# Gated cross-attention and ternary FFN on one Trainium2 core: quantised rows transposed by DMA in place of TensorE, a pipeline one tile deeper, and the down product in another place

## The chip, the cores and the metric

The kernel runs on one core of one Trainium2 chip. The metric is device microseconds per run. The kernel before takes 1334.1 us, the median of 3 runs (1331.85 to 1337.51). Five engines of the core work side by side, each through its own queue in order: TensorE (matrix products into PSUM), VectorE, ScalarE (activations), GpSimd, and SyncE, which issues the DMAs. They wait for one another on semaphores.

## The reference

x is 4 x 2048 x 512 in float32, the context 4 x 77 x 384; `g_xattn` and `g_ffn` are scalars.

```
x = x + tanh(g_xattn[0]) * xattn(layernorm(x), ctx)     # 8 heads of 64, keys 77, softmax; then @ Wo + bo
x = x + tanh(g_ffn[0])   * ffn(layernorm(x))

def act_quant(x):      # per row
    scale = 127 / clip(max|x|, 1e-5);  return clip(round(x * scale), -128, 127) / scale
def weight_quant(w):   # whole matrix, ternary
    scale = 1 / clip(mean|w|, 1e-5);   return clip(round(w * scale), -1, 1) / scale
bitlinear(x, w) = act_quant(x) @ weight_quant(w).T
g = bitlinear(x, w_gate); u = bitlinear(x, w_up)        # 512 -> 2048
h = relu(g)**2 * u
ffn = bitlinear(h, w_down)                               # 2048 -> 512
```

## The kernel before

The 8192 rows are 64 tiles of 128 rows, 16 tiles to a batch. A preparation makes the ternary weights (held in bf16, w_gate, w_up and w_down) and folds the query weights into the keys and the output weights into the values, batch by batch. Attention then is, for a tile: scores of 8 heads x 77 keys = 616 columns, softmax, five transposes of the probabilities, and a product with the folded values. Scores and attention run in float32r, each operand split into a high and a low part (24 score matmuls of 308 columns, 15 attention matmuls of 512). The FFN's quantised integers are exact in bf16.

The order is written out by hand. Each engine has a function `step(s)`, one for each tile t; `s.has(d)` guards the work for tile t+d, and a step treats several tiles at once. In the kernel before, TensorE's step is: gate and up of tile t, quarters 0 and 1; transposes of the probabilities of t+1 (L950); quarters 2 and 3 (L975); attention of t+1 (L962); three quarters of the scores of t+2 (L58); eight transposes of the first half of the marked hidden row (L983); the rest of the scores; the other eight; the down product (L1002) up to its last four matmuls; four transposes of the marked input of t+1 (L989); the last four of down. A quarter is 512 columns of gate and 512 of up, and its two banks of `gu_ps` alternate with those of the next quarter; the transposes also go to `gu_ps`.

ScalarE's step: relu (L870) and square (L874) of quarters 0 and 1, the high part of the transposed probabilities (L880), quarters 2 and 3, the high part of x (L841), `mark_hidden` (L891), `unmark_hidden` (L896), `mark_input` (L902), `exponentials` of t+2 (L863). Marking multiplies by the row's scale and adds a large constant, so that the rounded integer stands in the low half of the float32 word; the transposes on TensorE take these low halves as bf16, and unmarking subtracts the mark from the 16-bit integers in PSUM and writes bf16 for the next product.

VectorE's step: for each quarter the product with up (L1082) and its maximum (L1085); the low part of the probabilities (L1072); statistics (L1046); the hidden scales (L1091 to L1099); `add_attention` (L1106 on), `unmark_hidden` (L1139), `input_scale`, the maximum and the shift of the scores of t+2 (L1053, L1059), `unmark_input` (L1144), sum, reciprocal and normalisation of the probabilities of t+2 (L1063, L1065, L1068), and `finish` (L1151), which writes y. GpSimd does two roots (L820) and the low part of x (L803) in a step, and splits the folded keys and values at each change of batch (L809, L815). SyncE issues in a step the load of `xf_sb`, of `x_sb`, and the store of y.

Of the kernel before, what the change touches and what calls it, by code (L numbers as in the profile page):

```python
# [11 lines left out]
I16 = mybir.dt.int16  # L12

P = 128
# [7 lines left out]
PAIRS = TILES // 2  # L22
BATCH_PAIRS = TILES_PER_BATCH // 2
# [11 lines left out]
QUARTERS = FFN // 512  # L35
# [10 lines left out]
LOW_MARK = 16384.0  # L46
MARKED = ROUND + LOW_MARK

# [20 lines left out]
def gated_block(nc, x_tok, x_feat, ctx_t, wk, wv, wq_t, wo, bo, gates, wg_t, wu_t, wd_t, out, a_scr, v_scr):  # L69
# [7 lines left out]
    with ExitStack() as keep:  # L77
# [5 lines left out]
        kept.ident_b = sb("ident_b", [P, P], BF16)  # L83
# [37 lines left out]
def prepare(nc, x_tok, x_feat, ctx_t, wk, wv, wq_t, wo, bo, gates, wg_t, wu_t, wd_t, a_scr, v_scr, kept):  # L121
# [3 lines left out]
    ident_f, ident_b, neg_half, w_gate, w_up = kept.ident_f, kept.ident_b, kept.neg_half, kept.w_gate, kept.w_up  # L125
# [7 lines left out]
    with ExitStack() as ctx:  # L133
# [47 lines left out]
        ones_ready, zeros_ready, idents_zeroed = sem("ones_ready"), sem("zeros_ready"), sem("idents_zeroed")  # L181
        idents_ready = sem("idents_ready")
# [27 lines left out]
        with nc.Block() as block:  # L210
# [39 lines left out]
            @block.gpsimd  # L250
            def _(pool):
                nc.gpsimd.memset(ones[:, :], 1.0).then_inc(ones_ready, 1)
                nc.gpsimd.memset(k_pairs[:, :, :, :], 0.0).then_inc(zeros_ready, 1)
                nc.gpsimd.memset(v_pairs[:, :, :], 0.0).then_inc(zeros_ready, 1)
                nc.gpsimd.memset(neg_half[:, :], -0.5)
                nc.gpsimd.memset(ident_f[:, :], 0.0).then_inc(idents_zeroed, 1)
                nc.gpsimd.memset(ident_b[:, :], 0.0).then_inc(idents_zeroed, 1)
                pool.wait_ge(idents_zeroed, 2)
                for m in (ident_f, ident_b):
                    nc.gpsimd.affine_select(out=m[:, :], in_=m[:, :], compare_op=ALU.not_equal, fill=1.0, base=0,  # L260
                                            pattern=[[-1, P]], channel_multiplier=1).then_inc(idents_ready, 1)
# [294 lines left out]
def run_tiles(nc, x_tok, x_feat, out, a_scr, v_scr, kept):  # L556


    ident_f, ident_b, neg_half = kept.ident_f, kept.ident_b, kept.neg_half
# [7 lines left out]
    x_tok = x_tok.rearrange("(k o) p d -> k o p d", o=2)  # L567
    x_feat = x_feat.rearrange("(k o) p c t -> k o p c t", o=2)
    out = out.rearrange("(k o) p d -> k o p d", o=2)

    with ExitStack() as ctx:
# [3 lines left out]
        def sem(name):  # L575
# [11 lines left out]
        x1 = sb("x1", [P, 2, DIM], F32)  # L587
# [15 lines left out]
        hidden_scale = sb("hidden_scale", [P, 1], F32)  # L603
        x_marked = sb("x_marked", [P, DIM], F32)
        xq_t = sb("xq_t", [P, DIM], BF16)
        quarter_max = sb("quarter_max", [P, QUARTERS], F32)
# [4 lines left out]
        y_scale = sb("y_scale", [P, 1], F32)  # L611


        relu, relu_sq, y_sb = (staged[:, at:at + FFN // 2].rearrange("p (s n) -> p s n", s=2)
                               for at in (0, FFN // 2, 5 * FFN // 2))
        hidden = staged[:, FFN:2 * FFN]
        hq_t = staged[:, 2 * FFN:5 * FFN // 2].bitcast(BF16)
# [9 lines left out]
        ht_ps = [gu_ps[:, 0, n, :].bitcast(BF16) for n in range(2)]  # L627
        xt_ps = gu_ps[:, 1, 0, 0:DIM // 2].bitcast(BF16)
        x_bits = x_marked[:, :].bitcast(BF16).rearrange("p (n two) -> p n two", two=2)
        h_bits = h_marked[:, :].bitcast(BF16).rearrange("p (n two) -> p n two", two=2)  # L630
# [19 lines left out]
        xt_done, xq_ready = sem("xt_done"), sem("xq_ready")  # L650
        top_n_done, top_sq_done, hidden_scale_done = sem("top_n_done"), sem("top_sq_done"), sem("hidden_scale_done")
        gu_done = [sem(f"gu_done{n}") for n in range(QUARTERS)]
        relu_done = [sem(f"relu_done{n}") for n in range(QUARTERS)]
        square_done = [sem(f"square_done{n}") for n in range(QUARTERS)]
        hidden_done = [sem(f"hidden_done{n}") for n in range(QUARTERS)]
        quarter_max_done = sem("quarter_max_done")
# [3 lines left out]
        ht_done = [sem(f"ht_done{n}") for n in range(2)]  # L660
        hq_ready = [sem(f"hq_ready{n}") for n in range(2)]
# [5 lines left out]
        class Step:  # L667
# [3 lines left out]
            def __init__(self, eng, k, o, values=()):  # L671
                self.k, self.o, self.fixed = k, o, isinstance(k, int)
                self.held = {}
                if not self.fixed:
                    self.held = {c: 2 * k + (o + c) for c in values}
# [3 lines left out]
            def count(self, c):  # L679

                return self.held[c] if c in self.held else 2 * self.k + (self.o + c)
# [10 lines left out]
            def pair(self, d):  # L692
                return self.k + (self.o + d) // 2

            def loads(self, d):

                return 16 * self.pair(d) + 16

            def batch_chunks(self, d, chunks):

                return chunks * (self.pair(d) // BATCH_PAIRS) + chunks

            def opens(self, t):

                return self.fixed and 2 * self.k + self.o == t

            def has(self, d):
                return not self.fixed or 0 <= 2 * self.k + self.o + d < TILES

        SP_VALUES = (1, 2, 3)  # L710
# [5 lines left out]

        def steps(eng, step, values):

            for t in (-1, 0, 1):
                step(Step(eng, t // 2, t % 2))  # L720
            with eng.Fori(1, PAIRS - 2) as k:
                for o in range(2):
                    step(Step(eng, k, o, values))
            for t in range(TILES - 4, TILES):
                step(Step(eng, t // 2, t % 2))

        def steps_by_batch(eng, step, values, split_keys, split_values):

            for t in (-1, 0, 1):
                step(Step(eng, t // 2, t % 2))  # L730
            with eng.Fori(1, BATCH) as b:
                with eng.Fori(1, BATCH_PAIRS - 1) as k:
                    for o in range(2):
                        step(Step(eng, (b - 1) * BATCH_PAIRS + k, o, values))
                k = (b - 1) * BATCH_PAIRS + (BATCH_PAIRS - 1)
                split_keys(b)
                step(Step(eng, k, 0, values))
                split_values(b)
                step(Step(eng, k, 1, values))
                for o in range(2):  # L740
                    step(Step(eng, k + 1, o, values))
            with eng.Fori(PAIRS - BATCH_PAIRS + 1, PAIRS - 2) as k:
                for o in range(2):
                    step(Step(eng, k, o, values))
            for t in range(TILES - 4, TILES):
                step(Step(eng, t // 2, t % 2))

        with nc.Block() as block:
            @block.sync
            def _(sp):  # L750
# [8 lines left out]
                def load_xf(s, d):  # L759
                    sp.dma_start(xf_sb[:, s.par(d), :, :], x_feat[s.pair(d), s.par(d)]).then_inc(xf_loaded[s.par(d)], 16)  # L760

                def load_x(s, d):
                    sp.dma_start(x_sb[:, s.par(d), :], x_tok[s.pair(d), s.par(d)]).then_inc(x_loaded[s.par(d)], 16)

                def step(s):
                    if s.has(4):

                        sp.wait_ge(xf_low_done, s.through(2))
                        load_xf(s, 4)
                    if s.has(3):  # L770

                        sp.wait_ge(x1_done, s.through(1))
                        load_x(s, 3)
                    if s.has(0):

                        sp.wait_ge(x1_done, 1)
                        sp.wait_ge(y_done, s.through(0))
                        sp.dma_start(out[s.pair(0), s.par(0)], y_sb[:, s.par(0), :]).then_inc(y_stored[s.par(0)], 16)
# [3 lines left out]
                step(Step(sp, -1, 1))  # L782
                with sp.Fori(1, BATCH) as b:
                    load_folded(b)
                    with sp.Fori(0, BATCH_PAIRS) as k:
                        for o in range(2):
                            step(Step(sp, (b - 1) * BATCH_PAIRS + k, o, SP_VALUES))
                with sp.Fori(PAIRS - BATCH_PAIRS, PAIRS - 2) as k:
                    for o in range(2):
                        step(Step(sp, k, o, SP_VALUES))  # L790
                for t in range(TILES - 4, TILES):
                    step(Step(sp, t // 2, t % 2))
                for n in range(2):
                    sp.wait_ge(y_stored[n], 16 * PAIRS)

            @block.gpsimd
            def _(pool):
# [23 lines left out]

                def step(s):
                    if s.has(2):
                        root(var1_ready, s, 2, rstd1, var_eps1, rstd1_done)
                    if s.has(1):
                        root(var2_ready, s, 1, rstd2, var_eps2, rstd2_done)
                    if s.has(3):
                        low_part(s, 3)
# [3 lines left out]
                split_values(0)  # L832
                steps_by_batch(pool, step, (2, 3, 4), split_keys, split_values)

            @block.scalar
            def _(act):
# [28 lines left out]
                def square_quarter(s, n):  # L865
                    wait(act, gu_done[n], s.through(0))
# [3 lines left out]
                    nc.scalar.activation(relu[:, n % 2, :], gu_ps[:, n % 2, 0, :], ACT.Relu).then_inc(relu_done[n], 1)  # L870
                    wait(act, relu_done[n], s.through(0))

                    wait(act, hidden_done[(n + 2) % 4], s.count(1 if n >= 2 else 0))
                    nc.scalar.activation(relu_sq[:, n % 2, :], relu[:, n % 2, :], ACT.Square).then_inc(square_done[n], 1)  # L874
# [7 lines left out]
                def mark_hidden(s):  # L882
                    wait(act, h_scale_done, s.through(0))

                    wait(act, ht_done[1], s.before(0))
                    if s.opens(0):

                        wait(act, weight_done, PIECES)
                    for n in range(2):
                        cols = slice(n * FFN // 2, (n + 1) * FFN // 2)  # L890
                        nc.scalar.activation(h_marked[:, cols], hidden[:, cols], ACT.Copy, bias=MARKED,  # L891
                                             scale=h_scale[:, 0:1]).then_inc(h_marked_done[n], 1)

                def unmark_hidden(s):
# [344 lines left out]
```

## Time and profile before

| | before |
|---|---|
| median of 3 runs | 1334.1 us |
| lowest, highest | 1331.85, 1337.51 us |
| profiled execution: span, first to last instruction | 1332.6 us |
| busy TensorE | 1281.4 us, 96% |
| busy VectorE | 1123.8 us, 84% |
| busy ScalarE | 754.0 us, 57% |
| busy GpSimd | 199.7 us, 15% |
| mean granted TensorE clock | 0.990 |
| DMA traffic | 82.46 MB, mean 62 GB/s |

The profiled execution's own time is known by its span alone, which is 1.5 us under the median. The busy shares count instructions that overlap once. In the slices of the page, each of 40 equal parts of the span has a digit for the tenths that an engine is busy; PEclk is the TensorE clock that was granted, in tenths of full speed. A row of the timeline gives the start, the length and the instruction group, and in brackets the engine's idle time ahead of it with what ended it. Lengths of matmuls overlap: the start of one to the start of the next is what the engine spends.

### The profile page before, as it was taken

The page shows a single profiled execution, that of the slowest core. Times are in us where ns is not written, and L with a number is a line of the kernel's source. Part 1 is how long each engine was busy: PE and PEld are TensorE (multiplying, and loading weights), DVE is VectorE, ACT ScalarE, POOL GpSimd, SP SyncE. Part 2 cuts the span into 40 slices and gives each one's busy share as a digit, 9 for nine tenths or more (in the row PEclk, how much of TensorE's full clock was granted, in tenths as well). Part 3 has the DMA queues.
Part 4 walks back from the last instruction along what each step waited for, and adds up shares of the span by engine and source line. Part 5 has one row for each costly group of instructions (what it writes and reads, how often), then busy time and mean ns, then how long its engine had stood idle before and what let it go on. Part 6 is the DMA issues. An engine that isn't in the chain of part 4 may idle for free.

```text
span 1332.6 us, 21398 instructions
## 1 busy us (share of the span) xinstructions
PE 1281.4 (96%) x7289; PEld 848.3 (64%) x7416; DVE 1123.8 (84%) x2462; ACT 754.0 (57%) x1038; POOL 199.7 (15%) x216
## 2 busy tenths in 40 slices
PE   7768999999999999999999999999999999999996
PEld 5535666666666666666666666666666666666663
DVE  4969888888888888888888888888888888888885
ACT  3754555555566555555566555555566555555554
POOL 1022011101132111111122111111122110111000
PEclk9889999999999999999999999999999999999999
DMA  9732111111113111111112211111111111111100
GB/s 391 258 130 100 43 46 39 39 47 40 42 37 121 42 39 39 47 39 45 34 47 88 68 38 47 39 47 32 47 39 45 34 47 39 47 31 47 31 25 17
DMA packets 35188, 82.46 MB, mean 62 GB/s; under 512 B 3946, under 2 KB 3946, under 8 KB 32609
## 3 DMA queue, kind: packets, MB, share of 16 engines
q1 hardware_dynamic: 34589, 78.03, 17.2%
q10 hardware_dynamic: 580, 4.20, 1.0%
q8 instruction: 9, 0.15, 0.1%
q14 instruction: 10, 0.08, 0.0%
HBM read 57.86 MB, written 24.35 MB: 62 GB/s over the span
## 4 chain that ended last, share of the span: by engine, by line
PE 86%; DVE 3%; issue 2%; ACT 1%; POOL 0%; ACTq 0%; DVEq 0%; POOLq 0%
PE gu_ps L975 31%; PE o_ps L962 16%; PE y_ps L1002 16%; PE s_ps L58 16%; PE gu_ps L983 4%; PE s_ps L950 2%; PE gu_ps L989 1%; ACT v_sb L854 1%; DVE staged L1158 0%; ACT staged L891 0%; DVE probs L1059 0%; DVE staged L1082 0%; POOL v_sb L815 0%; DVE score_max L1053 0%; DVE w_down L1160 0%
## 5 line engine op out<-in xcount | busy, mean ns | idle before, releaser
L870 ACT ACTIVATE staged<-gu_ps 128x512 f32<-128x512 f32 x256 | 153.1, 598 | 230.9 <-PE gu_ps L975 230.5
L975 PE MATMUL gu_ps<-w_gate,xq_t 128*128 128x512 bf16 x961 | 259.3, 379 | 4.5 <-DVE xq_t L1144 0.9
L975 PE MATMUL gu_ps<-w_up,xq_t 128*128 128x512 bf16 x1024 | 262.8, 379 | 0.0
L1002 PE MATMUL y_ps<-w_down,staged 128*128 128x512 bf16 x960 | 228.5, 380 | 3.6 <-issue 0.2
L891 ACT ACTIVATE staged<-staged,h_scale 128x1024 f32<-128x1024 f32 x128 | 140.3, 1144 | 148.9 <-DVE h_scale L1098 148.9
L820 POOL TENSOR_TENSOR rstd<-var_eps,neg_half 128x1 f32<-128x1 f32 x128 | 74.1, 579 | 994.7 <-DVE var_eps L1048 647.0
L1082 DVE TENSOR_TENSOR staged<-staged,gu_ps 128x512 f32<-128x512 f32 x256 | 174.9, 683 | 53.1 <-ACT staged L874 53.0
L962 PE MATMUL o_ps<-v_sb,pt_high 128*128 128x512 f32 (+1 forms) x640 | 213.4, 415 | 3.4 <-DVE pt_low L1072 2.9
L58 PE MATMUL s_ps<-a_sb,xf_high 128*128 128x308 f32 x1024 | 191.4, 309 | 0.0
L1085 DVE TENSOR_REDUCE quarter_max<-staged 128x1 f32<-128x512 f32 x256 | 175.6, 686 | 8.8
L975 PEld LDWEIGHTS gu_ps<-w_up,xq_t 128*128 128x128 bf16 x1024 | 100.2, 98 | 120.8
L874 ACT ACTIVATE staged<-staged 128x512 f32<-128x512 f32 x256 | 161.7, 632 | 8.2
L975 PEld LDWEIGHTS gu_ps<-w_gate,xq_t 128*128 128x128 bf16 x1024 | 92.6, 97 | 111.5 <-DVE staged L1082 19.7
L58 PEld LDWEIGHTS s_ps<-a_sb,xf_high 128*128 128x128 f32 x1024 | 157.2, 188 | 5.8 <-issue 0.5
L1002 PEld LDWEIGHTS y_ps<-w_down,staged 128*128 128x128 bf16 x1024 | 95.0, 98 | 91.6 <-issue 1.0
L962 PEld LDWEIGHTS o_ps<-v_sb,pt_high 128*128 128x128 f32 (+1 forms) x640 | 121.1, 190 | 37.5 <-DVE pt_low L1072 3.2
L962 PE MATMUL o_ps<-v_sb,pt_low 128*128 128x512 f32 (+1 forms) x320 | 127.1, 397 | 0.0
L896 ACT ACTIVATE staged<-gu_ps 128x1024 bf16<-128x1024 int16 x64 | 65.5, 1024 | 101.4 <-PE gu_ps L983 101.4
L58 PE MATMUL s_ps<-a_sb,xf_low 128*128 128x308 f32 x512 | 113.3, 302 | 0.0
L983 PE MATMUL gu_ps<-ident_b,staged 128*128 128x128 bf16 x1024 | 80.4, 222 | 8.3 <-ACT staged L891 8.3
L58 PEld LDWEIGHTS s_ps<-a_sb,xf_low 128*128 128x128 f32 x512 | 84.5, 189 | 0.0
L803 POOL TENSOR_TENSOR xf_low<-xf_sb,xf_high 128x512 fp32r<-128x512 f32 x62 | 79.0, 1275 | 0.0
(112 smaller groups left out, 1509.3 us busy)
## 6 DMA issues: line engine op xcount, KB each, us to landing
xf_sb<-in_x_feat SPq DMA_DIRECT2D x64, 256.0 KB, 2.6
x_sb<-in_x_tok SPq DMA_DIRECT2D x64, 256.0 KB, 2.6
y<-staged SPq DMA_DIRECT2D x64, 256.0 KB, 2.0
staged<-in_wg_t SPq DMA_DIRECT2D x4, 1024.0 KB, 15.3
staged_up<-in_wu_t SPq DMA_DIRECT2D x4, 1024.0 KB, 23.2
staged<-in_wd_t ACTq DMA_DIRECT2D x4, 1024.0 KB, 7.1
a_scr<-a_out SPq DMA_DIRECT2D x12, 308.0 KB, 4.4
a_raw<-a_scr SPq DMA_DIRECT2D x3, 1232.0 KB, 5.3
```

The costliest lines, as they stand in the source:

```text
L58: last = nc.tensor.matmul(s_ps[:, n, 0:HALF_KEYS], x_part[:, c, :], a_sb[:, a, c, n * HALF_KEYS:(n + 1) * HALF_KEYS], start=(c == 0 and x_ ...
L803: nc.gpsimd.tensor_tensor(xf_low[:, s.par(d), :, :], xf_sb[:, s.par(d), :, :], xf_high[:, s.par(d), :, :].bitcast(F32), ALU.subtract).then ...
L820: nc.gpsimd.tensor_tensor(rstd[:, :], var_eps[:, :], neg_half[:, :], ALU.pow).then_inc(done, 1)
L870: nc.scalar.activation(relu[:, n % 2, :], gu_ps[:, n % 2, 0, :], ACT.Relu).then_inc(relu_done[n], 1)
L874: nc.scalar.activation(relu_sq[:, n % 2, :], relu[:, n % 2, :], ACT.Square).then_inc(square_done[n], 1)
L891: nc.scalar.activation(h_marked[:, cols], hidden[:, cols], ACT.Copy, bias=MARKED, scale=h_scale[:, 0:1]).then_inc(h_marked_done[n], 1)
L962: last = nc.tensor.matmul(o_ps[:, :], pt[0:rows, P * c:P * (c + 1)], v_sb[0:rows, v, c, :], start=(c == 0 and pt is pt_high and v == 0), s ...
L975: last = nc.tensor.matmul(gu_ps[:, n % 2, m, :], xq_t[:, P * c:P * (c + 1)], w[:, c, 512 * n:512 * (n + 1)], start=(c == 0), stop=(c == DC ...
L983: last = nc.tensor.transpose(ht_ps[n][:, P * c:P * (c + 1)], h_bits[:, at:at + P, 0], ident_b[:, :])
L1002: last = nc.tensor.matmul(y_ps[:, :], hq_t[:, P * c:P * (c + 1)], w_down[:, c, :], start=(c == 0), stop=(c == FC - 1))
L1082: nc.vector.tensor_tensor(hidden[:, cols], relu_sq[:, n % 2, :], gu_ps[:, n % 2, 1, :], ALU.mult).then_inc(hidden_done[n], 1)
L1085: nc.vector.tensor_reduce(quarter_max[:, n:n + 1], hidden[:, cols], axis=AX, op=ALU.max, apply_absolute_value=True).then_inc(quarter_max_d ...
```

## The change

Hidden row and input are no longer transposed on TensorE. Marking now adds `ROUND` alone; unmarking subtracts it from SBUF and writes bf16 rows (`hq` in halves, by VectorE and ScalarE; `xq` by VectorE); SyncE transposes these rows from SBUF to SBUF with `dma_start_transpose` (`turn_hidden`, two a tile, 128x1024 each; `turn_input`, one, 128x512) into `hq_t` and `xq_t`. The down product of a tile is in the step behind its gate and up (`down(s, -1)`), and `finish` in the one behind that (`finish(s, -2)`). `x1` becomes a ring of four, `hidden_scale`, `y_scale` and `xq_t` rings of two.

Gate and up come in two halves instead of four quarters. A half is 1024 columns of gate and then 1024 of up and fills the four banks of `gu_ps`; relu, square, product and maximum are one instruction a half. Relu waits for the gate product alone (`gate_done`), the product with up for `up_done`. The multiplication of the probabilities by the reciprocal sum goes from VectorE to GpSimd. Loops are unrolled over four tiles instead of two, and the split of keys and values at a change of batch stands two steps later in them.

```
 def gate_up(s, n):
+    wait(pe, hidden_done[1 - n], s.count(n))
+    for m, w, done in ((0, w_gate, gate_done), (1, w_up, up_done)):
+        for q in range(2):
+            cols = slice(HALF * n + 512 * q, HALF * n + 512 * (q + 1))
+            for c in range(DC):
+                last = nc.tensor.matmul(gu_ps[:, m, q, :], xq_t[:, s.par(0), c, :], w[:, c, cols], ...)
+        last.then_inc(done[n], 1)
 # TensorE
 def step(s):
-    gate_up(s, 0); gate_up(s, 1)
     transpose_probs(s, 1)
-    gate_up(s, 2); gate_up(s, 3)
+    gate_up(s, 0)
     attend(s, 1)
-    make_scores(s, 2, range(DC - 1)); transpose_hidden(s, 0); make_scores(s, 2, range(DC - 1, DC))
-    transpose_hidden(s, 1); down(s, range(FC - DC)); transpose_input(s, 1); down(s, range(FC - DC, FC))
+    make_scores(s, 2)
+    down(s, -1)
+    gate_up(s, 1)
 # ScalarE
 def step(s):
+    probs_high(s, 1); mark_hidden(s, -1)
+    relu_half(s, 0); square_half(s, 0)
+    unmark_hidden(s, -1); high_part(s, 3); mark_input(s, 1)
+    relu_half(s, 1)
+    exponentials(s, 2)
+    square_half(s, 1)
 # VectorE
 def step(s):
+    probs_low(s, 1); finish(s, -2); input_stats(s, 2); unmark_hidden(s, -1)
+    hidden_half(s, 0)
+    add_attention(s, 1); input_scale(s, 1)
+    top_scores(s, 2); unmark_input(s, 1); shift_scores(s, 2)
+    top_half(s, 0); hidden_unit_scale(s, 1); sum_probs(s, 2)
+    hidden_half(s, 1); top_half(s, 1); hidden_scales(s)
 # GpSimd
 def step(s):
     root(var1_ready, s, 2, ...)
+    low_part(s, 3)
     root(var2_ready, s, 1, ...)
-    low_part(s, 3)
+    normalise(s, 2)
 # SyncE
+def turn_hidden(s, d, n):
+    wait(sp, hq_done[n], s.through(d))
+    wait(sp, down_done, s.before(d))
+    sp.dma_start_transpose(hq_t[:, n * FC // 2:(n + 1) * FC // 2, :], hq[:, n * HALF:(n + 1) * HALF]).then_inc(hq_turned[n], 16)
+def turn_input(s, d):
+    wait(sp, xq_done, s.through(d))
+    wait(sp, up_done[1], s.before(d - 1))
+    sp.dma_start_transpose(xq_t[:, s.par(d), :, :], xq[:, :]).then_inc(xq_turned, 16)
 def step(s):
+    wait(sp, y_done, s.through(-2)); sp.dma_start(out[...], y_sb[:, s.par(-2), :])
+    turn_hidden(s, -1, 0); turn_hidden(s, -1, 1)
     load_xf(s, 4); load_x(s, 3)
+    turn_input(s, 1)
```

## Rows read from the trace of the kernel before

**Rows 1.** The page: busy us, share of span and instructions; granted clock in 40 slices.
```profile
PE 1281.4 (96%) x7289; PEld 848.3 (64%) x7416; DVE 1123.8 (84%) x2462; ACT 754.0 (57%) x1038; POOL 199.7 (15%) x216
...
PEclk9889999999999999999999999999999999999999
```

**Rows 2.** TensorE's timeline, 949 to 979 us: start us, us, instruction group.
```profile
954.10 0.71 PE L950 MATMUL s_ps<-ident_f,probs 128*128 128x128 f32 x5
954.64 1.03 PE L975 MATMUL gu_ps<-w_gate,xq_t 128*128 128x512 bf16 x4
...
957.23 1.03 PE L975 MATMUL gu_ps<-w_up,xq_t 128*128 128x512 bf16 x4
...
961.59 0.73 PE L58 MATMUL s_ps<-a_sb,xf_high 128*128 128x308 f32 x4
...
964.14 0.62 PE L983 MATMUL gu_ps<-ident_b,staged 128*128 128x128 bf16 x8
964.57 0.80 PE L58 MATMUL s_ps<-a_sb,xf_high 128*128 128x308 f32 x4
...
966.16 2.54 PE L1002 MATMUL y_ps<-w_down,staged 128*128 128x512 bf16 x11
968.54 0.39 PE L989 MATMUL gu_ps<-ident_b,x_marked 128*128 128x128 bf16 x4
...
973.08 0.71 PE L950 MATMUL s_ps<-ident_f,probs 128*128 128x128 f32 x5
```

**Rows 3.** ScalarE's and VectorE's timeline of the same stretch.
```profile
954.30 0.60 ACT L870 ACTIVATE staged<-gu_ps 128x512 f32<-128x512 f32 x1 [0.47 <-PE gu_ps L975]
...
962.36 2.19 ACT L891 ACTIVATE staged<-staged,h_scale 128x1024 f32<-128x1024 f32 x2 [2.28 <-DVE h_scale L1098]
...
968.29 0.81 ACT L863 ACTIVATE probs<-probs,rstd 128x616 f32<-128x616 f32 x1 [0.51 <-DVE probs L1059]
...
961.48 0.16 DVE L1091 TENSOR_REDUCE h_max<-quarter_max 128x1 f32<-128x4 f32 x1
...
969.87 0.79 DVE L1063 TENSOR_REDUCE prob_sum<-probs 128x8 f32<-128x616 f32 x1
970.69 0.20 DVE L1065 RECIPROCAL prob_inv<-prob_sum 128x8 f32<-128x8 f32 x1
```

**Rows 4.** Groups by line and form, whole run: busy us, mean ns; idle before, releaser.
```profile
L1082 DVE TENSOR_TENSOR staged<-staged,gu_ps 128x512 f32<-128x512 f32 x256 | 174.9, 683 | 53.1 <-ACT staged L874 53.0
L803 POOL TENSOR_TENSOR xf_low<-xf_sb,xf_high 128x512 fp32r<-128x512 f32 x62 | 79.0, 1275 | 0.0
L891 ACT ACTIVATE staged<-staged,h_scale 128x1024 f32<-128x1024 f32 x128 | 140.3, 1144 | 148.9 <-DVE h_scale L1098 148.9
L896 ACT ACTIVATE staged<-gu_ps 128x1024 bf16<-128x1024 int16 x64 | 65.5, 1024 | 101.4 <-PE gu_ps L983 101.4
L815 POOL TENSOR_TENSOR v_sb<-v_raw,v_sb 128x2048 fp32r<-128x2048 f32 x4 | 18.2, 4561 | 16.1 <-ACT v_sb L854 16.1
```

**Rows 5.** DMA view: packets, MB, engine share; issues with KB and us to landing.
```profile
q1 hardware_dynamic: 34589, 78.03, 17.2%
...
xf_sb<-in_x_feat SPq DMA_DIRECT2D x64, 256.0 KB, 2.6
...
y<-staged SPq DMA_DIRECT2D x64, 256.0 KB, 2.0
```

**Rows 6.** TensorE's timeline, first gate and up of the last tile.
```profile
1310.58 1.03 PE L975 MATMUL gu_ps<-w_gate,xq_t 128*128 128x512 bf16 x4
```

**Rows 7.** TensorE's timeline in the preparation; then windows (busy us of each engine, PEclk, DMA).
```profile
56.72 1.31 PE L287 MATMUL s_ps<-k_pairs,wq_sb 128*128 128x154 f32 x8 [1.91 <-ACT a_out L358]
...
76.68 7.54 PE L301 MATMUL v_ps<-wo_sb,v_pairs 128*128 128x512 f32 x13 [3.17 <-DVE v_pairs L464]
...
48.00:60.00 12.00, 8.95 (x43) 6.02 (x43) 11.82 (x13) 10.22 (x11) 0.00 (x0) 1.00 0.97 337
...
76.00:80.00 4.00, 3.32 (x5) 1.50 (x6) 1.90 (x11) 1.29 (x2) 0.56 (x1) 0.65 0.20 78
```

More of the change, by code:

```diff
@@ L626, in run_tiles @@
         pt_ps = s_ps[:, :, :].rearrange("p s n -> p (s n)")
[L627 to L630, printed above, removed]
+        gate_ps = gu_ps[:, 0, :, :].rearrange("p s n -> p (s n)")
+        up_ps = gu_ps[:, 1, :, :].rearrange("p s n -> p (s n)")
         v_parts = ((slice(0, P), slice(0, KC - 1)), (slice(0, LAST_ROWS + 1), slice(KC - 1, KC)))
@@ L674, in __init__ @@
                 if not self.fixed:
-                    self.held = {c: 2 * k + (o + c) for c in values}
+                    self.held = {c: QUAD * k + (o + c) for c in values}
                     for value in self.held.values():
@@ L744, in steps_by_batch @@
                     step(Step(eng, k, o, values))
-            for t in range(TILES - 4, TILES):
-                step(Step(eng, t // 2, t % 2))
+            last_steps(eng, step)
         with nc.Block() as block:
@@ L769, in step @@
                         load_xf(s, 4)
                     if s.has(3):
-                        sp.wait_ge(x1_done, s.through(1))
+                        wait(sp, x1_done, s.through(1))
                         load_x(s, 3)
[L774 to L778, printed above, removed]
+                    if s.has(1):
+                        turn_input(s, 1)
@@ L780, in _ @@
                 start = Step(sp, 0, 0)
                 load_xf(start, 2)
[L782 to L789, printed above, removed]
+                step(Step(sp, -1, QUAD - 1))
@@ new lines, in _ @@
+                for o in range(QUAD):
+                    step(Step(sp, 0, o))
+                    if o == 0:
+                        load_folded(1)
+                with sp.Fori(1, BATCH - 1) as b:
+                    with sp.Fori(1, BATCH_QUADS + 1) as j:
+                        for o in range(QUAD):
+                            step(Step(sp, (b - 1) * BATCH_QUADS + j, o, SP_VALUES))
+                    load_folded(b + 1)
+                with sp.Fori(QUADS - 2 * BATCH_QUADS + 1, QUADS - 1) as k:
+                    for o in range(QUAD):
@@ L968, in gate_up @@
                     if n == 0:
-                        wait(pe, xq_ready, s.through(0))
-                    if n >= 2:
-                        wait(pe, hidden_done[n - 2], s.through(0))
-                    for m, w in enumerate((w_gate, w_up)):
-                        for c in range(DC):
-                            last = nc.tensor.matmul(gu_ps[:, n % 2, m, :], xq_t[:, P * c:P * (c + 1)],
-                                                    w[:, c, 512 * n:512 * (n + 1)], start=(c == 0), stop=(c == DC - 1))
@@ L992, in down @@
-                def down(s, chunks):
-                    for n in range(2):
-                        if n * FC // 2 in chunks:
-                            wait(pe, hq_ready[n], s.through(0))
-                    if 0 in chunks:
-                        if s.opens(0):
-                            wait(pe, weight_done, PIECES)
-                        wait(pe, y_done, s.before(0))
-                    for c in chunks:
-                        last = nc.tensor.matmul(y_ps[:, :], hq_t[:, P * c:P * (c + 1)], w_down[:, c, :],
+                        wait(pe, xq_turned, s.turns(0))
@@ L1003, in down @@
+                def down(s, d):
+                    if s.opens(-d):
+                        wait(pe, weight_done, PIECES)
+                    wait(pe, y_done, s.before(d))
+                    for c in range(FC):
+                        for n in range(2):
+                            if c == n * FC // 2:
+                                wait(pe, hq_turned[n], s.turns(d))
+                        last = nc.tensor.matmul(y_ps[:, :], hq_t[:, c, :], w_down[:, c, :],
                                                 start=(c == 0), stop=(c == FC - 1))
-                    if FC - 1 in chunks:
-                        last.then_inc(down_done, 1)
+                    last.then_inc(down_done, 1)
@@ L1154, in ternary_down, with finish @@
+                def finish(s, d):
+                    wait(dve, down_done, s.through(d))
+                    wait(dve, y_scale_done, s.through(d))
+                    wait(dve, y_stored[s.par(d)], s.loads(d) - 16)
+                    nc.vector.scalar_tensor_tensor(y_sb[:, s.par(d), :], y_ps[:, :], y_scale[:, s.par(d):s.par(d) + 1],
+                                                   x1[:, s.ring(d), :], ALU.mult, ALU.add).then_inc(y_done, 1)
                 def ternary_down(p):
```

348 lines of the change are left out of this document (174 added, 174 removed).

## The prediction, made before the changed kernel ran

> **What bounds the kernel now.** I read the page's busy shares first: TensorE is busy 96% of the span, VectorE 84%, and behind the preparation (the first 110 us) TensorE's granted clock stays at 1.0 [rows 1]. A busy share does not say whether TensorE waits between its groups, so the timeline of one tile in the middle of the run came next [rows 2]. The probability transposes of one tile start at 954.10, those of the next at 973.08: 18.98 us a tile. The pieces, start to start: probability transposes 0.54 (954.10 to 954.64); half of gate and up 3.46 (954.64 to 958.10, where the four matmuls that start at 957.23 have been issued); attention 3.50 (958.10 to 961.59); scores 0.85 for six matmuls, 3.40 for 24; eight hidden transposes 0.43 (964.14 to 964.57), twice; down 16 x 0.217 = 3.48 (eleven take 2.38, from 966.16 to 968.54); four input transposes 0.22; the other half of gate and up 3.46. Their sum is 18.92, and 0.07 comes from breaking the scores in two. So TensorE has work without a hole, and 62 such steps make nearly the whole run. Everything else has slack: the exponential starts at 968.29 and the probabilities are wanted at 973.08 [rows 2, 3].
>
> **What is removed from the bound.** The 16 hidden and 4 input transposes, 0.86 + 0.22, and the break in the scores: TensorE's work falls to 0.54 + 3.46 + 3.50 + 3.40 + 3.48 + 3.46 = 17.84 us. Alone that is 1.14 us a tile. VectorE loses the normalisation (to GpSimd), about 0.8 us, and some fixed parts of instructions; it is not the bound before or after.
>
> **What the new order adds.** Number the step from the start of its probability transposes. TensorE does: transposes of tile t+1, 0.00 to 0.54; first half of gate and up of t, to 4.00; attention, to 7.50; scores of t+2, to 10.90; down of t-1, to 14.38; gate of the second half, to 16.11; up, to 17.84. Two things follow.
>
> First, ScalarE's queue has `relu_half(1)` ahead of `exponentials(2)`. The relu waits for the second gate product, at 16.11, though the scores were done at 10.90 and shifted by VectorE some 2.4 us later. Before, no wait on a late matmul stood there, the exponential waited 0.51 for its own input [rows 3]. Everything behind it is serial and the next step's first TensorE instruction, `transpose_probs`, waits for its end:
> - from the last gate matmul to the start of the relu 0.20 (954.10 against 954.30 in [rows 2, 3]);
> - relu over 128x1024 out of PSUM 1.02 (the row of 1024 elements out of PSUM, [rows 4]);
> - exponential 0.81, started 0.10 early as two of ScalarE's independent instructions overlap (two of 1.144 take 2.19), so 0.71 [rows 3, 4];
> - sum 0.04 + 0.78, reciprocal 0.04 + 0.20 [rows 3];
> - normalisation on GpSimd: no row has it. Its nearest rows are 128x512 in 1.275 and 128x2048 in 4.561, a slope of 2.14 ns an element, so 1.50 for 616 elements [rows 4]. From below it can't be under the 1.275 of fewer elements; from above I allow 2.0 for the broadcast operand. With 0.08 to start and 0.05 to TensorE: 1.63.
> Sum 4.62, so the next transposes start at 16.11 + 4.62 = 20.73. TensorE idles 2.9 us a step, and the step is 1.75 us longer than the 18.98 of before.
>
> Second, a half of gate and up now fills all four banks of gu_ps, where quarters alternated. So the first half of the next tile waits for `hidden_half(1)`: 0.20 + 1.02 + 0.71 + square 1.04 (1.144 less the overlap) + 0.04 + a product over 1024 elements (683 ns for 512, [rows 4], less one fixed part: 1.22) + 0.05 = 4.28, at 20.39. It hides behind the first loop, whose transposes end at 21.27, by 0.88. But had the first loop been free, this one would still give 20.39 - 0.54 = 19.85, slower than before.
>
> **The transposing DMAs.** SyncE issues three more transfers per tile, 256 KB twice and 128 KB, between the store of y and the loads; each such step holds SyncE behind waits for `hq_done`, `down_done` and `xq_done`, and the loads of x behind them, wanted a step later, have slack. When are they due? In the cycle of 20.73, the hidden maximum is done at 0.82, its scale 0.9 later (before, 961.48 to the ScalarE start at 962.36 [rows 3]), at 1.75. ScalarE marks until 3.94 (2.19), VectorE has the first half unmarked by about 5.1 (behind `probs_low`, `finish`, `input_stats`), ScalarE the second, behind relu and square, by about 7.0. Down wants the halves at 10.90 and 12.64. So each transfer has about 5.7 us. The input is ready near 12.5 and wanted at 21.27: 8.8 us. No row shows a transposing transfer. From below: the plain ones of the same bytes take 2.0 to 2.6 us from issue to landing. From above: 78 MB went in 34589 packets that took 17.2% of 16 x 1332.6 us, 106 ns each for 2.3 KB [rows 5]; if every 256-byte row of a transpose cost as much, a half is 1024 / 16 x 106 ns = 6.8 us of all engines and two in a row land near 20.5, which would hold down, and the step, by 7.9 us. I take 4 us, nearer the plain row because the bytes are the same and the engines are 83% idle; then nothing is late.
>
> The Trainium skill ("DMA: Bandwidth & Descriptors", Latency and other measured facts) gives transposing transfers an effective 261 GB/s, some 1.0 us for a half behind a fixed 2 us: by that rule nothing is late either. Against the change speaks "Advanced Engine Details and Errata" (DGE: Hardware vs Software) of the Trainium skill, which calls hardware-generated transposes the less efficient ones; it has no figure, and no row here tests it. It stands beside rival B.
>
> **The ends.** 62 steps at +1.75 are +108. At the three changes of batch GpSimd's split of the values (over 4.6 us and the last chunk behind it, [rows 4]) now starts at about 0.8 of the step whose attention starts at 4.0, not a whole gate and up ahead: about +2.5 each, +8. Input 0 comes through a DMA: +3. Behind the last gate and up the deeper pipeline has a whole down (of tile 62), the second half, and then marking, unmarking, transfer, down, finish and store in a row: I get 31.5 from the start of the last tile's gate and up, where before it was 1332.6 - 1310.6 = 22.0 [rows 6]: +9.5; one short step before it -1.5. Sum +127 on the span of 1332.6: 1460. The runs' median is 1334.1, 1.5 above the span.
>
> **TensorE's clock.** The waits that I add are 2.9 us. Before, after a wait of 3.17 that ended at 76.68 the granted clock is 0.65 over 76 to 80, so 1.2 in place of 2.4 GHz for 2.8 of 4 us; with a wait of 1.91 that ended at 56.72 it stays at 1.00 over 48 to 60 [rows 7]. 2.9 lies between, nearer the side that fell. A fall costs half of the stretch at half speed, over 1.4 us; I take 1.6. From never to every step that is 0 to +99 us; I take a third of the steps, +31. Forecast: 1460 + 31 + 1.5 = 1492 us.
>
> The Trainium skill ("TensorE: Matmul & The Clock Gate", Why this matters for your kernels) warns of idle gaps between bursts of matmuls in mid-kernel. Read strictly, that is rival F; the rows show one gap on either side and leave it open.
>
> **The rivals.** A measurement of this kernel tells 0.5%, about 7 us, from no change.
> - A, the forecast (52%): the softmax tail sets the step, the clock falls in some steps, 1440 to 1530.
> - F, the clock falls in every step (12%): 2.9 us of idle come once a step, and each is enough. 1460 + 62 x 1.6 + 1.5 = 1560. For it the wait that ended at 76.68, against it the one that ended at 56.72 [rows 7].
> - B, transfers late (18%): the transposed halves of the hidden rows land after 12.64, down stands, and as down lies in front of the second gate product, each us later is 62 us. It decides from 5.7 us after the issue. 1.5 us too late: 1492 + 93 = 1585. For it: 256-byte rows, and no measured one; against it: idle engines.
> - C, bound by TensorE, faster (8%): TensorE stays without holes at 17.84 and the removed transposes are kept. It needs the tail behind the second gate product to be no longer than the 1.73 of the up product, not 4.62: the exponential not held up. 1332.6 - 62 x 1.14 + 20 = 1282, where 20 is the ends' 19 and the 1.5 beside the span. Against it: the in-order queue of ScalarE, the four full banks. The side turns at a step of 18.98 - 20/62 = 18.66, a tail of 2.5 us.
> - D (2%): the two cancel, 1327 to 1341.
> - E (8%): only a part of the tail: GpSimd's piece shorter or semaphores quicker, no fall of the clock, 1341 to 1440.
> That the transposes leave TensorE is sure; that they were its bound is too. What is lost is worth more.
>
> Chances: faster 0.08, same 0.02, slower 0.90. The range, 1420 to 1600, leaves out C, D and the far part of B.
>
> **What would show it.** In the timeline after: idle of about 2.9 us before the probability transposes, released by GpSimd's normalisation; a step of 20.7 us where the clock stays at 1.0; the exponential starting right behind a relu of 1.0 us, with ScalarE waiting about 4 us for the gate product; gaps of the granted clock in some steps; no wait of down for a DMA. If down waits for hq_t, B holds. If TensorE's idle ends with VectorE's product in place of GpSimd's, the second loop binds and the step is 19.9. If TensorE is above 98% busy with steps of 17.9, the whole argument is wrong. Clock gaps in every step speak for F, none at all for a run near 1461.

## The result

The changed kernel takes 1465.4 us, median of 4 runs (1464.61 to 1468.81), beside 1335.3 for the kernel before; the ratio is 1.0989, 95% interval 1.0964 to 1.1015. It is 10% slower. The forecast was 1492 us, 12% slower, in a range of 1420 to 1600.

The page of the changed kernel, in the same columns as [rows 1]; the last two lines are its chain of waits, by engine, and its transposing transfers:

```profile
span 1466.9 us, 18673 instructions
...
PE 1237.2 (84%) x6040; PEld 782.6 (53%) x6136; DVE 1064.9 (73%) x2142; ACT 694.0 (47%) x782; POOL 306.3 (21%) x278
...
PEclk9979999999999999999999999999999999999997
...
PE 39%; issue 34%; DVE 11%; POOL 7%; ACT 2%; DMA 1%; DVEq 0%; POOLq 0%; ACTq 0%; SPq 0%
...
hq_t<-staged SPq DMA_TRANSPOSE x128, 3.0
```

TensorE does 44 us less than before and takes 134 us longer: its share falls from 96 to 84%. The chain of waits puts 34% on "issue" and 7% on GpSimd. "Issue" names no cause: it is time for which the chain shows no wait, in a plain step mostly some 8.4 us ahead of GpSimd's normalisation. The waits say more. The two longest waits of TensorE in the changed kernel (us in total, times, longest):

```profile
PE s_ps L1001 <- POOL probs L863: 170.9, 64, 12.2
PE y_ps L1041 <- DMA hq_t<-staged: 14.3, 4, 9.2
```

All 64 tiles wait for GpSimd's normalisation; for a DMA down waits in 4 only. The timeline of one step, TensorE first, then ScalarE, VectorE, GpSimd, to set beside [rows 2, 3]:

```profile
954.56 0.77 PE L1001 MATMUL s_ps<-ident_f,probs 128*128 128x128 f32 x5 [2.45 <-POOL probs L863]
955.16 1.89 PE L1028 MATMUL gu_ps<-w_gate,xq_t 128*128 128x512 bf16 x8
...
965.51 3.63 PE L1041 MATMUL y_ps<-w_down,hq_t 128*128 128x512 bf16 x15
968.98 1.89 PE L1028 MATMUL gu_ps<-w_gate,xq_t 128*128 128x512 bf16 x8
970.70 1.89 PE L1028 MATMUL gu_ps<-w_up,xq_t 128*128 128x512 bf16 x8
...
970.90 1.02 ACT L916 ACTIVATE staged<-gu_ps 128x1024 f32<-128x1024 f32 x1 [4.23 <-PE gu_ps L1028]
971.83 0.80 ACT L909 ACTIVATE probs<-probs,rstd 128x616 f32<-128x616 f32 x1
972.52 1.04 ACT L922 ACTIVATE staged<-staged 128x1024 f32<-128x1024 f32 x1
...
967.14 0.79 DVE L1087 TENSOR_TENSOR probs<-s_ps,score_max 128x616 f32<-128x616 f32 x1
...
972.66 0.80 DVE L1091 TENSOR_REDUCE prob_sum<-probs 128x8 f32<-128x616 f32 x1 [3.02 <-ACT probs L909]
973.49 0.20 DVE L1093 RECIPROCAL prob_inv<-prob_sum 128x8 f32<-128x8 f32 x1
...
973.77 1.22 POOL L863 TENSOR_TENSOR probs<-probs,prob_inv 128x616 f32<-128x616 f32 x1 [8.45 <-DVE prob_inv L1093]
...
975.04 0.77 PE L1001 MATMUL s_ps<-ident_f,probs 128*128 128x128 f32 x5 [2.45 <-POOL probs L863]
```

Read it backwards from 975.04, the next step's start. The normalisation ends at 974.99, started at 973.77 behind the reciprocal, that behind the sum, that behind the exponential at 971.83. The exponential's input was ready at 967.93; it started 3.9 us later because ScalarE stood in front of the relu, 4.23 us, for the last gate matmul, which ends at 970.70. From there to 975.04 is 4.34 us, of which the up product covers 1.73. The step is 975.04 - 954.56 = 20.48. TensorE's idle ahead of the transposes, 2.45 us by its row, is called the hole below.

Over the run, the starts of the probability transposes give the account of the 134.3 us. Plain steps are the 52 behind the first two in which no batch changes:

| | before | after | difference |
|---|---|---|---|
| start to first transposes | 97.4 | 101.0 | +3.6 |
| first two steps | 39.7 | 38.1 | -1.5 |
| 52 plain steps | 18.98 each | 20.48 each | +78.0 |
| 3 changes of batch, 3 steps each | 172.2 | 208.7 | +36.5 |
| from the last transposes to the end | 36.4 | 54.1 | +17.7 |

### The profile page after: what moved, and what is told of

Read it like the earlier page. It is cut to its first block, busy times and chain, and to the rows that moved or that the text cites. A ratio compares the mean times of both kernels' runs of the same rounds, so it can differ in the third digit from the quotient of the medians.

```text
span 1466.9 us, 18673 instructions
## 1 busy us (share of the span) xinstructions
PE 1237.2 (84%) x6040; PEld 782.6 (53%) x6136; DVE 1064.9 (73%) x2142; ACT 694.0 (47%) x782; POOL 306.3 (21%) x278
## 4 chain that ended last, share of the span: by engine, by line
PE 39%; issue 34%; DVE 11%; POOL 7%; ACT 2%; DMA 1%; DVEq 0%; POOLq 0%; ACTq 0%; SPq 0%
PE o_ps L1013 15%; PE gu_ps L1028 15%; POOL probs L863 5%; PE s_ps L1001 3%; PE y_ps L1041 3%; DVE stats L1137 3%; DVE x L1135 3%; PE s_ps L56 2%; POOL rstd L858 2%; DVE centred L1141 2%; POOL v_sb L853 1%; DVE mean_var L1067 1%; ACT staged L922 1%; ACT v_sb L900 1%; DMA hq_t<-staged 1%
## 5 line engine op out<-in xcount | busy, mean ns | idle before, releaser
L916 ACT ACTIVATE staged<-gu_ps 128x1024 f32<-128x1024 f32 x128 | 130.1, 1016 | 276.7 <-PE gu_ps L1028 276.5
L1041 PE MATMUL y_ps<-w_down,hq_t 128*128 128x512 bf16 x962 | 228.4, 385 | 18.3 <-DMA hq_t<-staged 14.3
L1107 DVE TENSOR_TENSOR staged<-staged,gu_ps 128x1024 f32<-128x1024 f32 x128 | 156.0, 1219 | 70.9 <-ACT staged L922 70.9
L1001 PE MATMUL s_ps<-ident_f,probs 128*128 128x128 f32 (+1 forms) x320 | 51.9, 296 | 170.9 <-POOL probs L863 170.9
L863 POOL TENSOR_TENSOR probs<-probs,prob_inv 128x616 f32<-128x616 f32 x64 | 78.8, 1231 | 529.6 <-DVE prob_inv L1093 529.6
L1091 DVE TENSOR_REDUCE prob_sum<-probs 128x8 f32<-128x616 f32 x64 | 50.9, 795 | 190.4 <-ACT probs L909 190.4
L952 ACT ACTIVATE x_marked<-centred,x_scale 128x512 f32<-128x512 f32 x64 | 46.2, 722 | 268.3 <-DVE x_scale L1154 268.3
L1041 PEld LDWEIGHTS y_ps<-w_down,hq_t 128*128 128x128 bf16 x1024 | 96.1, 99 | 130.5 <-issue 19.1
L1112 DVE TENSOR_REDUCE half_max<-staged 128x1 f32<-128x1024 f32 x128 | 155.4, 1214 | 2.2
L922 ACT ACTIVATE staged<-staged 128x1024 f32<-128x1024 f32 x128 | 134.8, 1053 | 2.2
```

What stands on the lines that cost most here:

```text
L863: nc.gpsimd.tensor_tensor(probs_by_head, probs_by_head, inv, ALU.mult).then_inc(probs_ready, 1)
L916: nc.scalar.activation(relu, gate_ps, ACT.Relu).then_inc(relu_done[n], 1)
L922: nc.scalar.activation(relu_sq, relu, ACT.Square).then_inc(square_done[n], 1)
L1001: last = nc.tensor.transpose(pt_ps[0:cols, P * c:P * (c + 1)], probs[:, P * c:P * c + cols], ident_f[:, :])
L1041: last = nc.tensor.matmul(y_ps[:, :], hq_t[:, c, :], w_down[:, c, :], start=(c == 0), stop=(c == FC - 1))
L1107: nc.vector.tensor_tensor(hidden[:, cols], relu_sq, up_ps, ALU.mult).then_inc(hidden_done[n], 1)
```

## The experiments

Theory 1: the order makes two loops, chains that leave TensorE at the second gate product and come back to it, one through the softmax tail and one through the four full banks of `gu_ps`; the removed transposes were worth their full price. Rivals: the transposing transfers; VectorE's long list; the clock.

**The down product behind the second half.** One move in TensorE's step:

```
-    if s.has(-1): down(s, -1)
     if s.has(0):  gate_up(s, 1)
+    if s.has(-1): down(s, -1)
```

> The changed kernel with the down product of the tile before moved behind the second half of gate and up. Theory 1 (the softmax tail behind the second gate product sets the step of 20.48 us, because only the up product of 1.73 us lies beside it): 3.48 us of down now lie beside that tail too, 1.73 + 3.48 is more than the 4.34 that the tail takes, so TensorE has no hole left in plain steps, the step is about 17.9 us and the run 1300 to 1325. Rival (the time went into the transposing DMAs, or into VectorE with its long in-order list): the step stays above 19 us, the run above 1380.

Measured: 1290.0 us, ratio to the kernel before 0.9657 (0.9634 to 0.9680). Plain steps are 17.81 us, the 17.84 that I had added up for TensorE's work. TensorE and GpSimd of this kernel, and a window of one step (us busy of TensorE, its weight loads, VectorE, ScalarE, GpSimd; granted clock):

```profile
871.32 1.90 PE L1028 MATMUL gu_ps<-w_gate,xq_t 128*128 128x512 bf16 x8
873.06 1.89 PE L1028 MATMUL gu_ps<-w_up,xq_t 128*128 128x512 bf16 x8
874.79 3.62 PE L1041 MATMUL y_ps<-w_down,hq_t 128*128 128x512 bf16 x16
878.24 0.71 PE L1001 MATMUL s_ps<-ident_f,probs 128*128 128x128 f32 x5
...
876.38 1.22 POOL L863 TENSOR_TENSOR probs<-probs,prob_inv 128x616 f32<-128x616 f32 x1 [5.34 <-DVE prob_inv L1093]
...
860.40:878.20 17.80, 17.80 (x93) 11.52 (x92) 15.11 (x33) 9.71 (x11) 4.00 (x4) 1.00 0.32 81
```

The normalisation ends at 877.60, 4.54 behind the gate product's end (4.29 in the changed kernel), and 0.64 ahead of the transposes that want it. The same tail is there; down covers it. VectorE's list, 15.11 us, fits. The transfers, the deeper pipeline and the halves are all in this kernel too, and it is faster than the kernel before: without the down product in its place ahead of the second half, none of them makes the kernel slow.

**The exponential ahead of the second relu.**

```
+    if s.has(2): exponentials(s, 2)
     if s.has(0): relu_half(s, 1)
-    if s.has(2): exponentials(s, 2)
```

> The changed kernel with the exponential ahead of the second relu in ScalarE's queue. Theory 1: the exponential starts some 3 us earlier and the probabilities are ready in time; then the second loop binds, relu, square and product of the second half before the next gate product may write the same four banks: the last gate matmul at 16.1, the next first half at 19.7, a step of 19.2 us, the run about 1390. Rival (GpSimd's normalisation alone was late, and the banks cost nothing): 17.9 us a step, 1310. Rival (ScalarE's order is without effect): 1465.

Measured: 1398.9 us, ratio 1.0478 (1.0453 to 1.0503), steps of 19.26. TensorE's timeline has the wait at the place of the second loop, ahead of the first gate product, released by VectorE's product, and none before the transposes:

```profile
870.41 1.89 PE L1028 MATMUL gu_ps<-w_up,xq_t 128*128 128x512 bf16 x8
872.14 0.71 PE L1001 MATMUL s_ps<-ident_f,probs 128*128 128x128 f32 x5
874.13 1.89 PE L1028 MATMUL gu_ps<-w_gate,xq_t 128*128 128x512 bf16 x8 [1.28 <-DVE staged L1107]
```

So the move takes 20.48 - 19.26 = 1.22 us off the step, and the banks hold the other 1.45 down to 17.81. The 1.22 is not the price of the softmax tail alone: the exponential ahead of the relu is out of the second loop too, so both loops got shorter.

**Work put into the hole, and in front of it.** Five matmuls more per tile, 1.08 us, the price of the transposes that were removed: once in the up product of the second half, once in its gate product.

```
 for q in range(2):
+    if n == 1 and m == 1 and q == 1:         # m == 0 in the second kernel
+        for c in (0, 1, 2, 3, 0):
+            nc.tensor.matmul(gu_ps[:, m, q, :], xq_t[...], w[:, c, cols], start=True, stop=True)
```

> The changed kernel with five more matmuls of 512 columns in every second half, in the up product behind the last gate matmul (1.08 us a tile, as much as the transposes that left TensorE; their result is overwritten). Theory 1: they fall into TensorE's hole, the time stays within 0.5% of the changed kernel, 1465. Rival (TensorE's work still counts): up to 64 x 1.08 = 69 us more, 1534.

> The same five matmuls in the gate product of the second half, ahead of the semaphore that releases the relu. Theory 1: this work lies on the loop, so all of it shows: 60 x 1.08 = 65 us more, about 1530. Rival (a hole absorbs it wherever it stands): 1465.

Measured: 1463.6 us behind the gate, steps of 20.48 unchanged; 1587.0 ahead of its end. The first shows that 1.08 us of TensorE's work a tile, as much as was saved, is worth nothing at that place of this order. The second is 122 us more where 65 were expected. In its timeline the hole is as long as ever, but two kinds of step stand side by side, 21.55 and 23.24 (the transposes that open four steps, and windows over two of them with the granted clock in the last column but two):

```profile
1004.73 0.80 PE L1001 MATMUL s_ps<-ident_f,probs 128*128 128x128 f32 x5 [2.44 <-POOL probs L863]
1027.97 0.76 PE L1001 MATMUL s_ps<-ident_f,probs 128*128 128x128 f32 x5 [2.44 <-POOL probs L863]
1051.20 0.77 PE L1001 MATMUL s_ps<-ident_f,probs 128*128 128x128 f32 x5 [2.44 <-POOL probs L863]
1072.75 0.77 PE L1001 MATMUL s_ps<-ident_f,probs 128*128 128x128 f32 x5 [2.44 <-POOL probs L863]
...
1051.20:1072.80 21.60, 19.15 (x98) 11.98 (x98) 15.10 (x33) 9.71 (x11) 4.00 (x4) 1.00 0.26 67
1028.00:1051.20 23.20, 20.76 (x97) 12.33 (x97) 15.14 (x33) 9.71 (x11) 4.03 (x4) 0.93 0.26 62
```

The longer step has the clock at 0.93 of its 23.2 us, 3.2 us at 1.2 GHz, and is 1.69 longer. Of the 52 plain steps 32 are such, 54 us, nearly all of the missing part.

**A third transfer.** 128x1024 more transposed per tile into a tile that nothing reads, ahead of the two:

```
 if n == 0:
+    wait(sp, spare_turned, s.turns_before(d))
+    sp.dma_start_transpose(spare_t[:, :, :], hq[:, 0:HALF]).then_inc(spare_turned, 16)
+    sp.wait_ge(spare_turned, s.turns(d))       # in the second kernel only
```

> The changed kernel with a third transposing transfer of 128x1024 per tile, of the same rows into a tile that nothing reads, queued ahead of the two of the hidden row. In the changed kernel a transfer lands 3.0 us after issue and SyncE spends some 1.4 us on each; down begins 5.3 us after the first issue. Theory 1 (the transfers are hidden, slack over 2 us): it delays the two by about 1.4 us and the time stays within 0.5% of 1465. Rival (the transfers are on the path, by their engines or by contention in SBUF): 1.4 us a tile, 1550.

> The same third transfer, and SyncE waits for its landing before it issues the two: a delay of 3.0 us. Theory 1 with the slack as read (first half lands at 8.6 of the step and is due at 10.9, the second at about 10.2 and due at 12.7): down waits some 0.5 to 0.9 us a tile, 1495 to 1525. Rival (there is more slack): 1465. Rival (already on the path): 3 us a tile, 1650.

Measured: 1472.5 without the wait (ratio 1.1047, 1.1016 to 1.1079), 0.5% above the changed kernel, where 1.4 us a tile would be 6%; plain steps are 20.48 as before. So the transfers of the hidden rows, and half as many again, stay hidden in plain steps. The last 0.5% is at the edge of what the runs can tell. Of the 3.3 us between the two profiled executions 3.2 lie behind the last probability transposes (57.3 us against 54.2), where down has to wait for its transfers. With the wait 1548.3, outside what I expected. TensorE's waits of that kernel:

```profile
PE s_ps L1009 <- POOL probs L871: 169.7, 64, 12.2
PE y_ps L1049 <- DMA hq_t<-staged: 59.2, 40, 12.4
```

Its steps are 21.24 where the clock stays up, +0.76, within the 0.5 to 0.9 read from the slack; but 31 of the 52 plain steps are longer, up to 22.36, with the clock at half speed 27 times between 170 and 1490 us; the changed kernel has no such plain step. The slack was right, the clock was again what I had left out.

**The normalisation back on VectorE.**

```
 nc.vector.reciprocal(prob_inv, prob_sum)
+nc.vector.tensor_tensor(probs_by_head, probs_by_head, inv, ALU.mult)     # and out of GpSimd's step
```

> The changed kernel with the multiplication by the reciprocal sum back on VectorE, behind the reciprocal. Theory 1: the softmax tail gets shorter by 0.4 us (about 0.84 in place of 1.23 and two hand-offs), but the product of the second half, which VectorE does next, starts 0.84 later and frees the banks at the moment at which the first half of the next tile starts now: the second loop takes over, the step stays 20.4 to 20.6 us, the run 1455 to 1475. Rival (GpSimd's share of the tail counts in full): 20.0 us, 1435.

Measured: 1496.2 us, ratio 1.1213 (1.1185 to 1.1242): slower, where no change was expected. The timeline has the second loop behind the first, as reasoned: a wait before the transposes, then 0.45 more for VectorE's product.

```profile
604.31 0.77 PE L998 MATMUL s_ps<-ident_f,probs 128*128 128x128 f32 x5 [1.99 <-DVE probs L1093]
605.53 1.89 PE L1025 MATMUL gu_ps<-w_gate,xq_t 128*128 128x512 bf16 x8 [0.45 <-DVE staged L1107]
...
624.96 0.77 PE L998 MATMUL s_ps<-ident_f,probs 128*128 128x128 f32 x5 [1.99 <-DVE probs L1093]
```

The step is 20.65, +0.17, 9 us over the 52. The rest is the clock: 20 of the 52 plain steps are longer, most 22.3 or 21.8, 28 us in all. These 37 us are more than the 27.6 between the profiled executions, because this kernel reaches its first transposes at 92.2 us instead of 101.0.

**One matmul more.** Three kernels with longer steps had falls of the clock in plain steps, the changed kernel had none. In two of the three its hole was nearly unchanged (2.44 us, and 1.99 with 0.45 behind it); in the one with the waited transfer, waits of down came beside it. The diff is the one above with m == 0 and `for c in (0,)`.

> The changed kernel with one more matmul of 512 columns (0.22 us) in the gate product of the second half. TensorE's hole stays 2.45 us a step, only the step gets longer, 20.70. Theory 3 (in the changed kernel the hole never met a fall of the granted clock in a plain step because its step of exactly 20.48 us keeps the hole at the same place of whatever is watched; with another step length falls come, each 1.7 us, as in the runs with 21.56 and 20.65): falls in 15 to 30 steps, 1505 to 1530. Rival (the length of the hole alone decides): no falls, 1465 + 14 = 1479.

Measured: 1486.5 us, ratio 1.1137 (1.1113 to 1.1161), between the two expectations and in neither. Of the 52 plain steps 45 are 20.70 and 7 are 22.38: falls come, though fewer than I said. So the hole's length does not decide alone; with the same 2.44 to 2.45 us of waiting, a step of 20.48 had none in 52, one of 20.70 had 7, one of 21.55 had 32. But a longer step does not simply bring more: with the normalisation on VectorE and a step of 20.65 it was 20 of 52. That the meeting of hole and step length is the cause fits these numbers, but what the chip watches is not shown.

**The kernel before with few transposes.** Here the order of before stays, and the transposed rows and inputs are incomplete:

```
-for c in range(FC // 2):   # transpose_hidden; and range(DC) in transpose_input
+for c in range(1):         # full in the first tile
```

> The kernel before with 3 of its 20 bf16 transposes on TensorE per tile (one of each group, all of them in the first tile only), so that the rest of the transposed hidden row and input is left out of the computation. It shows what taking them off TensorE is worth when the order stays. Theory 1 (TensorE has no hole before): 17 transposes at 0.054 us are 0.92 us a tile, the step falls from 18.98 to about 18.05 us, the run to 1276. Rival (the chain of marking, unmarking and down, or VectorE, binds as soon as they are gone): above 1310.

Measured: 1280.1 us, ratio 0.9598 (0.9574 to 0.9622), steps of 18.12: 0.86 us less for 17 transposes, where 0.92 was expected. In the old order the transposes are worth nearly what they cost.

**VectorE held by GpSimd.** At each change of batch the changed kernel has three long steps, 23.58, 23.34 and 22.04 us at the first. VectorE's and GpSimd's timeline there:

```profile
407.06 0.21 DVE L1126 TENSOR_SCALAR h_scale<-h_inv,hidden_scale 128x1 f32<-128x1 f32 x1
407.19 4.42 DVE L1127 TENSOR_TENSOR y_scale<-h_top,down_unit 128x1 f32<-128x1 f32 x1
411.53 0.81 DVE L1097 TENSOR_TENSOR pt_low<-s_ps,pt_high 128x640 fp32r<-128x640 f32 x1
...
406.17 5.42 POOL L847 TENSOR_TENSOR a_sb<-a_raw,a_sb 128x2464 fp32r<-128x2464 f32 x1 [0.88 <-ACT a_sb L893]
...
412.39 0.74 PE L1013 MATMUL o_ps<-v_sb,pt_high 128*128 128x512 f32 x2 [2.83 <-DVE pt_low L1097]
435.74 0.72 PE L1013 MATMUL o_ps<-v_sb,pt_high 128*128 128x512 f32 x2 [2.59 <-POOL v_sb L853]
```

A product of one column takes 4.42 us, 0.15 in plain steps, and ends with GpSimd's split; so it does at each of the three changes (4.42, 4.41, 4.40, and 3.69 to 3.70 a step later, beside the split of the values). The instruction just ahead, with a scalar operand in place of the second tensor, takes 0.21 with GpSimd as busy. The edit and the two kernels with it:

```
-nc.vector.tensor_tensor(y_scale[...], h_top[:, :], down_unit[:, :], ALU.mult)
+nc.vector.tensor_scalar(y_scale[...], h_top[:, :], down_unit[:, 0:1], None, ALU.mult)
```

> The changed kernel with y_scale made by tensor_scalar (down_unit as its scalar) in place of tensor_tensor of two SBUF columns. In the changed kernel this 128x1 product takes 4.4 us instead of 0.15 while GpSimd splits the keys of the next batch, and 3.7 us while it splits the values. Theory 2 (a VectorE product of two SBUF operands waits for GpSimd's long one): the first of the two long steps of each change of batch falls from 23.6 to about 20.7 us, the second stays long because attention then waits for the split itself; 9 us less, 1456. Rival (every VectorE instruction would be held there): 1465.

> The down product behind the second half and y_scale by tensor_scalar. The step of 17.81 us has no hole, so the held instruction costs 3.8 us in the first long step of each change of batch (21.66, 20.14, 21.68 as read): about 9 to 11 us less than with the order alone, 1280. Rival (the splits cost GpSimd or attention the same anyway): 1290.

Measured: 1452.7 us, ratio 1.0888 (1.0860 to 1.0916), and with the down product last 1282.5, ratio 0.9610 (0.9587 to 0.9633). In the first the same stretch reads

```profile
407.33 0.20 DVE L1127 TENSOR_SCALAR y_scale<-h_top,down_unit 128x1 f32<-128x1 f32 x1
...
409.93 2.40 DVE L1170 TENSOR_SCALAR staged<-staged 128x1024 bf16<-128x1024 f32 x1
...
406.31 5.46 POOL L847 TENSOR_TENSOR a_sb<-a_raw,a_sb 128x2464 fp32r<-128x2464 f32 x1 [0.88 <-ACT a_sb L893]
...
433.23 0.73 PE L1013 MATMUL o_ps<-v_sb,pt_high 128*128 128x512 f32 x2 [3.04 <-POOL v_sb L853]
```

The first long step is gone (20.49), the second stays (23.79) with attention waiting for the split, and the third, which ran in part at half clock, is 20.48. The three steps together are 4.2 to 5.9 us shorter at each change of batch, 14 us in all. The second kernel, 7.5 us under the one with the down product last where 9 to 11 were expected, is the fastest that computes the whole reference: 3.9% under the kernel before. The Trainium skill ("SBUF — State Buffer", SBUF: two separate sides) says that VectorE and GpSimd share a pair of ports under an exclusive lock, which a VectorE instruction with two SBUF inputs contends for when the GpSimd instruction reads SBUF. The rows agree: 4.42 us with two, 0.20 with one. But one input alone does not free an instruction: the unmarking of the first half, 0.69 us elsewhere, takes 2.40 beside the same split and ends 0.6 behind it, at all three changes of batch.

## Why the prediction was right, step by step

- TensorE's work of 17.84 us: right, 17.81 in the kernel with down last. That its transposes were its bound: right, by the kernel before with few of them.
- The softmax tail behind the second gate product: right in place and order. I priced it at 4.62; it is 4.34. The term that was off is GpSimd's normalisation: 1.23 us against 1.50, below even the 1.275 which I took for its floor. That row is a subtraction that writes float32r; which difference makes it longer no run shows. A row of another form gave no floor here. Step 20.48 against 20.73.
- The second loop, 19.85 if alone: 19.26 as measured with the exponential first. My tail of 4.28 had 0.71 for the exponential ahead of the square; without it 3.57, and 874.13 - 870.41 = 3.72 was measured.
- The transfers: 3.0 us each where I took 4, due after 5.3 and more. Rival B is out: with a third one the plain steps stay at 20.48.
- Clock: wrong. I priced falls in a third of the steps at +31 us. None came in plain steps; the few (around the changes of batch and at the end) are in those rows of the account. The price of one, 1.6, was right (1.69). The forecast without falls, 1461, was closer, but by luck: I had taken the length of the wait to decide, and with nearly the same wait and a step of 20.65 or 20.70, shorter than the 20.73 of the forecast, 20 and 7 falls do come.
- Changes of batch: +8 forecast, +23 beyond the 1.50 that each of the nine steps is longer anyway. The late split of the values was right (2.59 to 3.0 us of waiting); the held y_scale was not in the sum at all, nor the clock after it.
- The ends: +11 forecast, +19.8 in the account. Down of tile 62 waits 3.55 us for its transfer and that of tile 63 9.22, where the row of mark, unmark and transfer has nothing beside it; the kernel before waits 4.86 there, for ScalarE, where 9.22 stands now. I had the pieces too short, and no clock in them: the granted clock is 0.83 over these 54.2 us, 0.95 over the 36.4 of before.

The errors of step length (-17 us: 108 forecast, 61 steps at 1.50 measured), clock (-31), batches (+15) and ends (+9) come to -24; the median stands 1.5 under the profiled span where I had added 1.5, -3 more. That is the whole of 1465 - 1492 = -27. Each of the four is more than can be told from no change, and two of them offset the other two by half, so a part of the closeness is luck.

## What to carry to other kernels

Taking work off the bound engine pays only if the order still covers the longest chain that leaves that engine and comes back. Find in the new order the last matmul before each such chain and the independent work issued between it and the chain's return: here 1.73 us against 4.34, and 5.2 after the move of one product. In an in-order queue, put nothing that waits for a late product ahead of something that is ready.

## What the runs showed of the hardware

- A wait of 2.45 us per step on TensorE went with a fall of the granted clock to half in none, 7 or 32 of 52 plain steps, with steps of 20.48, 20.70 and 21.55 us, 1.69 us a time. In the last, and with the normalisation back on VectorE (20 of 52), the falls cost 54 and 28 us that no sum of instructions showed.
- A VectorE product of two SBUF columns was held until GpSimd's product of SBUF operands ended (4.42 us for 0.15); with a scalar operand it was not (0.20), while a one-input subtraction from float32 to bf16 was (2.40 for 0.69).
- A transposing transfer of 128x1024 bf16, SBUF to SBUF, lands 3.0 us after its issue and 128x512 after 2.4; SyncE's rows show 1.2 to 1.4 us for each.
